# Second messages of a graph network: gathering features by chunk, and passing them through DRAM

## The chip, the cores and the metric

The kernel runs on one core of a Trainium2 chip. The metric is the device time of one execution in microseconds, lower is better. Engines: PE multiplies matrices, DVE (vector), ACT (scalar) and POOL (GpSimd) work on tiles, SP issues transfers. Sixteen DMA engines move data between DRAM and on-chip tiles; queue q1 is SP's, q10 ACT's, q0 POOL's.

## The reference

Two graph layers run over 12500 nodes with 160 features each (64 scalars and 32 vectors of three) and 212500 edges. The second one, cut to its messages:

```python
w = relu(edge_feature @ W_fc1) @ W_fc2            # (E, 224), five blocks
xs, xv = s[dst], v[dst]                           # gathered features: 64 and 32x3
tp = concat([w0 * xs, w3 * dot(xv, sh1), (w1 * xs) x sh1, w2 * xv, w4 * cross(xv, sh1)])
agg = segment_sum(tp, src, num_segments=N) / 32   # (N, 480)
```

Then `agg` goes through small matrices, a skip term and gates, and is added to x.

## The kernel before

Earlier stages sort the edges by the node that they are summed into. For each edge they leave one row of 229 words in `sorted_rows1` in DRAM (224 weights, three of direction, the key, and the index of the node whose features it needs), and for each node one row of 160 words in `feat_tab1`. After sorting, the rows of a block of 128 nodes lie together.

`messages(nc, t, l, g)` is used for both layers; the change is for the second, `L1`. It works in 928 steps (`NST`). A step takes 256 rows (`ST`), two for each of 128 partitions, from a row that a table names (`first_row`): a step never mixes blocks, so steps start at rows that aren't multiples of 256, and at the latest at 256 times their number. The steps are written out in turns of 12 (`TURN`), and a loop goes over the turns.

- SP (`group`): once in four steps (`GROUP`) it waits until the accumulation that is 8 steps back is done, reads four first rows from the table, and issues four loads of 256 rows into `rows`, a ring of 12 (`HELD`). Each load's pattern is given through `lanes(..., WIDE_LANES)`, which puts a dimension of 8 outermost.
- POOL (`gather`, L1506): for each step it waits for the rows and for a free slot in `feat`, a ring of 6 (`RING`), and issues two indirect DMAs of 128 rows of 640 B from `feat_tab1`, one for each of the step's two rows of a partition, with the indices in the rows.
- DVE: makes a one-hot matrix of the node within the block (L1790), one step later multiplies weights with features into `prod` (L1800, L1807), and adds PE's result to the accumulator (L1865) two steps after that.
- ACT: scales the one-hot by the three components of the direction (L1622), and issues stores of finished blocks to `agg_tab` (L1701) when a flag in a table says so.
- PE: 16 matmuls a step, scaled one-hots times products (L1601).

In code, the parts that the change touches:

```python
def lanes(a, n):
    return a.rearrange("(b a) w -> a b w", a=n)

sp.dma_start(rows[slot][:, :, :],
             lanes(g.sorted_rows[l.n][bass.ds(first[n], ST), :].rearrange(
                 "(p k) w -> p (k w)", k=ST_TILES), WIDE_LANES)).then_inc(rows_here[slot], 16)
```

Of the kernel before, what the change touches and what calls it, by code (L numbers as in the profile page):

```python
# [18 lines left out]
F32 = mybir.dt.float32  # L19
# [32 lines left out]
HELD = 12  # L52
GROUP = 4
TABLE_AT = 32
STORE_LAG = 10
NST = N_EDGES // ST + NBLK
HST = NST // 2
# [11 lines left out]
DIGITS = 6  # L69
TABLE_STEPS = 18  # L70
WIDE_LANES, SMALL_LANES = 8, 4
assert TURN % GROUP == 0 and NST % GROUP == 0 and HELD % GROUP == 0
assert PER_TURN % 2 == 0 and MID % 2 == 0 and NBLK + BLOCK_LAG <= MID_STEPS + 2 and NCHUNK % SLOTS == 0
assert NHI * NLO >= NBIN and NCOL % PIECE == 0
# [73 lines left out]
def build(nc, t, out):  # L148
    est = ExitStack()
    g = Shared()  # L150
    with est:
        def sb(name, shape, dt, ctx=est):
            return ctx.enter_context(nc.sbuf_tensor(name, shape, dt))

        def sem(name, ctx=est):
            return ctx.enter_context(nc.semaphore(name))

        def dram(name, shape, dt):
            return nc.dram_tensor(name, shape, dt, kind="Internal").ap()

        g.ps = [est.enter_context(nc.psum_tensor(f"bank{i}", [P, 512], F32)) for i in range(2)]
        g.ps2 = [est.enter_context(nc.psum_tensor(f"pair{i}", [P, 2, 512], F32)) for i in range(3)]

        g.sorted_rows = [dram(f"sorted_rows{l.n}", (E_PAD, l.width), I32) for l in (L0, L1)]
        g.feat_tab = [dram(f"feat_tab{l.n}", (N_PAD, D), F32) for l in (L0, L1)]
        g.agg_tab = [dram(f"agg_tab{l.n}", (N_TAB, l.agg), F32) for l in (L0, L1)]
        g.skip_tab = dram("skip_tab", (N_PAD, sum(L1.skip_cols)), F32)


        g.x_sb = sb("x_sb", [P, NBLK, D], F32)  # L170
        g.attr_s = sb("attr_s", [P, 3, NBLK], F32)
        g.ident = sb("ident", [P, P], F32)
        g.iota_n = sb("iota_n", [P, P], F32)
        g.ones_f = sb("ones_f", [P, P], F32)
        g.lower_bf = sb("lower_bf", [P, P], BF16)
        g.upper_bf = sb("upper_bf", [P, P], BF16)
        g.iota_bin = sb("iota_bin", [P, NBIN], BF16)
        g.tri = sb("tri", [P, CHUNK_TILES, CHUNK_TILES], BF16)
        g.before_f = sb("before_f", [P, P], F32)
        g.upto_f = sb("upto_f", [P, P], F32)  # L180
        g.eps = sb("eps", [P, 1], F32)
        g.w1 = [sb(f"fc1_{l.n}", [2 * l.fc_in, P], F32) for l in (L0, L1)]
        g.w2 = [sb(f"fc2_{l.n}", [P, l.wnum], F32) for l in (L0, L1)]
        g.wn_s = [sb(f"node_s{l.n}", [S0, S0 + l.skip_cols[0]], F32) for l in (L0, L1)]
        g.wn_v = [sb(f"node_v{l.n}", [V0, V0 + l.skip_cols[1]], F32) for l in (L0, L1)]
        g.w_out = [sb(f"w_out{l.n}", [P, len(l.kchunks), l.out_cols], F32) for l in (L0, L1)]
        g.neg_cross = sb("neg_cross", [32, 32], F32)
        fields = sb("fields", [TABLE_AT + 1, -(-(NST + STORE_LAG) // GROUP) * GROUP, 2], I32)
        g.first_row = fields[0:1, :, :].rearrange("p u c -> p (u c)")[:, 0:NST]
        g.table = fields[TABLE_AT:TABLE_AT + 1, :, :]  # L190
        g.fields = fields
        g.base_node = sb("base_node", [P, NST], F32)
        g.same_block = sb("same_block", [P, NST], F32)
        g.count_c = [sb(f"count_c{n}", [NHI * NLO, 1], F32) for n in range(2)]
        g.bin_start = [sb(f"bin_start{n}", [1, NBIN], F32) for n in range(2)]


        g.hi1 = sb("hi1", [P, NCOL + CHUNK_TILES], BF16)

        g.passed = sem("passed")  # L200
        g.feat_here = [[sem(f"feat_here{s}_m{l.n}") for s in range(RING)] for l in (L0, L1)]
        g.rows_sent = [sem(f"rows_sent{s}") for s in range(SLOTS)]
        g.sent = [[sem(f"sent{h}_{where}") for h in range(2)] for where in ("m0", "c")]
        sort_edges(nc, t, g)
        messages(nc, t, L0, g)
        middle(nc, t, g)
        messages(nc, t, L1, g)
        node_sums1(nc, out, g)

# [1196 lines left out]
def messages(nc, t, l, g):  # L1406
# [3 lines left out]
    with ExitStack() as ctx:  # L1410
# [3 lines left out]
        def sem(name):  # L1414
            used.append(nc.alloc_semaphore(f"{name}_m{l.n}"))
            return used[-1]

        sends = l.n == 0
        rows = [sb(f"rows{s}", [P, ST_TILES, l.width], I32) for s in range(HELD)]
        feat = [sb(f"feat{s}", [P, ST_TILES, D], F32) for s in range(RING)]  # L1420
        hot = [sb(f"hot{s}", [P, ST_TILES, 1 if sends else 4, P], F32) for s in range(l.hot_bufs)]
        prods = l.prod_bufs
        prod = [sb(f"prod{s}", [P, ST_TILES, l.pw], F32) for s in range(prods)]
        acc = [sb(f"acc{s}", [P, l.agg], F32) for s in range(l.accs)]
        rows_here = [sem(f"rows_here{s}") for s in range(HELD)]
        feat_here = g.feat_here[l.n]
        acc_stored = [sem(f"acc_stored{s}") for s in range(l.accs)]
        hot_ready, hot_scaled, prod_ready, sum_ready, acc_ready, iota_made = (
            sem(x) for x in ("hot_ready", "hot_scaled", "prod_ready", "sum_ready", "acc_ready", "iota_made"))
        if sends:  # L1430
            part = [sb(f"part{s}", [P, ST_TILES, S0 + V0], F32) for s in range(2)]
            part_ready, inner_ready, outer_ready = (sem(x) for x in ("part_ready", "inner_ready", "outer_ready"))
            scaled, made = outer_ready, inner_ready
            later = [sb(f"later{h}", [P, CHUNK_TILES, L1.width], I32) for h in range(2)]
            meta = [sb(f"meta{h}", [P, CHUNK_TILES, L1.meta], I32) for h in range(2)]
            turned = [sb(f"turned{h}", [2 * L1.fc_in, HALF * P], F32) for h in range(2)]
            hT = [sb(f"hT{h}", [P, HALF * P], F32) for h in range(2)]
            place = [sb(f"place{h}", [P, CHUNK_TILES], I32) for h in range(2)]
            sq = sb("sq", [P, CHUNK_TILES, 3], F32)
            dist = [sb(f"dist{n}", [P, CHUNK_TILES], F32) for n in range(3)]  # L1440
            turned_here = [sem(f"turned_here{h}") for h in range(2)]
            meta_here = [sem(f"meta_here{h}") for h in range(2)]
            sent = g.sent[0]
            hid_ready, hT_ready, w_ready, evicted, norm, root_ready, inverse, copied = (
                sem(x) for x in ("hid_ready", "hT_ready", "w_ready", "evicted", "norm", "root_ready", "inverse", "copied"))
            iota = g.ps2[1][:, 1, 0:P]
            r = rank_buffers(L1, sb, sem, g, g.ps2[2][:, 0, :], g.hi1, place, PER_TURN, iota=iota[:, 0:NBIN])
            hid = g.ps2[2][:, 1, :]
            w_bank = {i: g.ps2[0][:, n % 2, :] for n, i in enumerate(PAIRS)}
            res = [b[:, 0:l.agg].rearrange("p (o c) -> p o c", o=1)  # L1450
                   for b in (g.ps[0], g.ps[1], g.ps2[1][:, 0, :])]
        else:
            scaled, made = hot_scaled, prod_ready
            iota = g.ps[0][:, 0:P]
            res = [g.ps2[2 - s][:, :, 0:l.agg // 2] for s in range(l.res_bufs)]
# [23 lines left out]
        def _(sp):  # L1479
            def group(step, it, s):  # L1480
# [9 lines left out]
                for n in range(GROUP):  # L1490
# [1 line left out]
                    sp.dma_start(rows[slot][:, :, :],  # L1492
                                 lanes(g.sorted_rows[l.n][bass.ds(first[n], ST), :].rearrange(
                                     "(p k) w -> p (k w)", k=ST_TILES), WIDE_LANES)).then_inc(rows_here[slot], 16)
            turns(sp, STEPS, TURN, group, upto=NST // TURN)

        @block.gpsimd
        def _(pool):
            def gather(step, it, s):
                u = it * TURN + s  # L1500
                pool.wait_ge(rows_here[s % HELD], 16 * (use(it, s, HELD) + 1))
                if step is None or step >= RING:
                    pool.wait_ge(prod_ready, u - RING + 1)
                settle(pool, g.passed)
                for k in range(ST_TILES):
                    pool.indirect_dma_start(  # L1506
                        out=feat[s % RING][:, k, :], out_offset=None, in_=g.feat_tab[l.n],
                        in_offset=bass.IndirectOffsetOnAxis(ap=rows[s % HELD][:, k, l.idx_at:l.idx_at + 1], axis=0)
                    ).then_inc(feat_here[s % RING], 16)

            def send(step, it, s):

# [13 lines left out]
                        in_=later[h][:, k, :], in_offset=None).then_inc(sent[h], 16)  # L1526

            def step_(step, it, s):
                if step is None or step < NST:
                    gather(step, it, s)  # L1530
                if sends and (step is None or step >= 6):
                    send(step, it, s)
            turns(pool, STEPS, TURN, step_, tail=6 if sends else 0, upto=NST // TURN)
            if sends:
                for h in range(2):
                    pool.wait_ge(sent[h], CHUNK_TILES * 16 * (NCHUNK0 // 2))
# [188 lines left out]
        def _(dve):  # L1725
# [87 lines left out]
            def first_products(step, it, s):  # L1813
                u = it * TURN + s
                w, f, scalars, vectors = forms(s)
                dve.wait_ge(feat_here[s % RING], 16 * ST_TILES * (use(it, s, RING) + 1))
                if step is None or step >= prods:
                    dve.wait_ge(sum_ready, u - prods + 1)
                if sends:
# [296 lines left out]
```

## Time and profile before

| | us |
|---|---|
| median of 3 runs | 9462.45 (9452.29 to 9468.72) |
| the profiled execution | 9444.39 |
| its span, first to last instruction | 9442.3 |
| the second messages' gathers, first to last start | 6846.8 to 9237.0 |

Busy shares over the whole span: PE 70%, DVE 76%, POOL 73%, ACT 52%. They mix stages with different limits, so the rows below are mostly of one stage.

### The profile page before, as it was taken

Reading aid. Unit: us, or ns where it says so; the run is one execution under the profiler, and the core shown is the slowest. Engines: PE = TensorE matmul, PEld = TensorE weight load, DVE = VectorE, ACT = ScalarE, POOL = GpSimd, SP = SyncE. Lnnn points to the kernel's source line nnn. Section 1 sums busy time; section 2 is a strip of 40 time slices with the busy share of each in tenths; the row PEclk is TensorE's granted clock in tenths of the full one; section 3 lists DMA queues with packets and bytes.
Section 4 is the critical chain, followed back from the end, with each engine's and each line's share of the span. In section 5 each row is a group of like instructions: output and inputs, shape, how many; then the busy total and the mean of one; then the engine's idle time right before and its main releaser. Section 6 shows DMA issues by size and latency. Waiting matters only on the chain. (4 is left out here: it accounts for less than half of the span.)

```text
span 9442.3 us, 170962 instructions
## 1 busy us (share of the span) xinstructions
PE 6603.2 (70%) x31166; PEld 4445.8 (47%) x31166; DVE 7219.4 (76%) x21240; ACT 4946.3 (52%) x16490; POOL 6911.8 (73%) x7069
## 2 busy tenths in 40 slices
PE   5666566655565555555565555578799999999999
PEld 3333333332222222222222222246588888888888
DVE  7666666665777777777777777767799999999996
ACT  3444444443444444444444444444477777777775
POOL 5777777777777777777777777766677777777771
PEclk7556555657888888888888888889899999999999
DMA  3222222224444444444444444445556666666667
GB/s 105 93 91 93 92 92 93 91 90 123 139 139 140 138 138 139 139 139 139 138 139 139 139 139 139 136 143 174 158 167 168 169 169 168 170 171 167 170 166 231
DMA packets 826471, 1315.58 MB, mean 139 GB/s; under 512 B 228521, under 2 KB 627625, under 8 KB 826281
## 3 DMA queue, kind: packets, MB, share of 16 engines
q0 software_dynamic: 337920, 667.48, 25.2%
q1 hardware_dynamic: 417496, 547.30, 19.3%
q10 hardware_dynamic: 70992, 100.14, 3.1%
q8 instruction: 20, 0.33, 0.0%
q14 instruction: 43, 0.34, 0.0%
HBM read 862.45 MB, written 914.08 MB: 188 GB/s over the span
## 5 line engine op out<-in xcount | busy, mean ns | idle before, releaser
L1506 POOL DMA_INDIRECT feat_m<-feat_tab,rows_m x3712 | 3638.3, 980 | 1155.8 <-issue 984.9
L1634 ACT ACTIVATE prod_m<-part_m,rows_m 128x64 f32<-128x64 f32 x5568 | 1432.4, 337 | 2136.1 <-DVE part_m L1824 1940.3
L1601 PE MATMUL pair<-prod_m,hot_m 128*128 128x160 f32 x14848 | 2246.6, 305 | 158.1 <-DVE prod_m L1807 121.7
L1582 PE MATMUL bank<-prod_m,hot_m 128*128 128x449 f32 x2476 | 1322.6, 665 | 1438.8 <-DVE prod_m L1844 1287.6
L1601 PEld LDWEIGHTS pair<-prod_m,hot_m 128*128 128x128 f32 x14848 | 2045.5, 190 | 359.3 <-issue 354.2
L1622 ACT ACTIVATE hot_m<-hot_m,rows_m 128x128 f32<-128x128 f32 x5568 | 1728.6, 389 | 693.6 <-DVE hot_m L1790 687.6
L659 POOL DMA_INDIRECT sorted_rows<-rows_e,place_e x1664 | 1611.1, 968 | 540.9 <-issue 505.5
L1582 PEld LDWEIGHTS bank<-prod_m,hot_m 128*128 128x128 f32 x2476 | 534.4, 231 | 2169.0 <-issue 2003.6
L1524 POOL DMA_INDIRECT sorted_rows<-later_m,place_m x1248 | 1229.5, 985 | 385.5 <-issue 371.0
L1807 DVE TENSOR_TENSOR prod_m<-rows_m,feat_m 128x192 f32<-128x192 f32 (+2 forms) x4640 | 1319.0, 323 | 0.0
L1865 DVE SCALAR_TENSOR_TENSOR acc_m<-acc_m,same_block,pair 128x640 f32<-128x640 f32 (+1 forms) x1237 | 1033.4, 835 | 3.4 <-PE pair L1601 3.4
L1824 DVE TENSOR_TENSOR part_m<-rows_m,feat_m 128x128 f32<-128x128 f32 x928 | 268.1, 289 | 939.9 <-DMA feat_m<-feat_tab,rows_m 938.1
L1800 DVE TENSOR_TENSOR prod_m<-rows_m,feat_m 128x128 f32<-128x128 f32 x2784 | 726.5, 293 | 96.0 <-DMA feat_m<-feat_tab,rows_m 94.6
L1582 PE MATMUL pair<-prod_m,hot_m 128*128 128x449 f32 x1236 | 548.8, 567 | 166.0 <-DVE prod_m L1844 165.5
L484 PE MATMUL pair<-fc,hT_e 64*128 64x192 f32 x3328 | 602.6, 539 | 0.4 <-ACT rows_e L688 0.4
L412 PE MATMUL bank<-bin_count_e,upper_bf 128*128 128x100 bf16 x207 | 53.7, 259 | 779.7 <-DVE bin_prod_e L346 779.7
L484 PEld LDWEIGHTS pair<-fc,hT_e 64*128 64x128 f32 x3328 | 500.0, 325 | 198.0 <-issue 197.9
L796 DVE COPY first_sh_e<-meta_e 128x8 f32<-128x8 f32 x208 | 35.9, 173 | 701.3 <-DMA sorted_rows<-rows_e,place_e 698.9
L1115 POOL DMA_INDIRECT sorted_rows<-later_c,place_c x416 | 425.8, 1024 | 191.2 <-issue 135.3
L686 ACT ACTIVATE rows_e<-pair,first_sh_e 128x96 f32<-128x96 f32 x1664 | 499.5, 371 | 121.5 <-PE pair L484 121.5
L676 ACT ACTIVATE hT_e<-bank 128x512 f32<-128x512 f32 x208 | 124.2, 597 | 701.5 <-PE bank L929 700.4
L1790 DVE SCALAR_TENSOR_TENSOR hot_m<-pair,base_node,rows_m 128x256 f32<-128x256 f32 x928 | 445.6, 480 | 30.6 <-issue 21.4
(263 smaller groups left out, 9893.8 us busy)
## 6 DMA issues: line engine op xcount, KB each, us to landing
agg_tab<-acc_m ACTq DMA_DIRECT2D x928, 320.0 KB
rows_m<-sorted_rows SPq DMA_DIRECT2D x928, 229.0 KB
agg_tab<-acc_m ACTq DMA_DIRECT2D x928, 224.5 KB
rows_m<-sorted_rows SPq DMA_DIRECT2D x928, 197.0 KB
feat_m<-feat_tab,rows_m POOLq DMA_INDIRECT x3712, 2.7
turned_m<-in_turned ACTq DMA_DIRECT2D x159, 256.0 KB
agg_s<-agg_tab SPq DMA_DIRECT2D x98, 320.0 KB, 4.0
sorted_rows<-rows_e,place_e POOLq DMA_INDIRECT x1664, 2.4
```

The costliest lines, as they stand in the source:

```text
L484: return pe.matmul(out, hT[h, k % HALF * P:(k % HALF + 1) * P], g.w2[l.n][h, :], start=True, stop=True)
L659: pool.indirect_dma_start(out=g.sorted_rows[0], out_offset=bass.IndirectOffsetOnAxis(ap=place[s][:, k:k + 1], axis=0), in_=rows[s][:, k, : ...
L686: act.activation(rows_f[:, 2 * i + k, 0:96], w[:, k, 0:96], ACT.Copy, scale=first_sh[s][:, 2 * i + k, :])
L1506: pool.indirect_dma_start(out=feat[s % RING][:, k, :], out_offset=None, in_=g.feat_tab[l.n], in_offset=bass.IndirectOffsetOnAxis(ap=rows[s ...
L1524: pool.indirect_dma_start(out=g.sorted_rows[1], out_offset=bass.IndirectOffsetOnAxis(ap=place[h][:, k:k + 1], axis=0), in_=later[h][:, k, ...
L1582: mm = pe.matmul(out[:, 0, :], hot[s % l.hot_bufs][:, k, 0, :], prod[s % prods][:, k, 0:l.agg], start=(k == 0), stop=(k == ST_TILES - 1))
L1601: mm = pe.matmul(dst, hot[s % l.hot_bufs][:, k, q, :], rhs, start=(k == 0 and q < 2), stop=(k == ST_TILES - 1), skip_group_check=True)
L1622: ins = act.activation(hot[s % l.hot_bufs][:, k, 1 + q, :], hot[s % l.hot_bufs][:, k, 0, :], ACT.Copy, scale=rows[s % HELD][:, k, l.sh_at ...
L1634: ins = act.activation(prod[s % prods][:, k, at:at + S0], part[s % 2][:, k, 0:S0], ACT.Copy, scale=rows[s % HELD][:, k, l.sh_at + m:l.sh_a ...
L1800: return dve.tensor_tensor(out_p[:, :, pcol:pcol + 64 * d].rearrange("p k (q c) -> p k q c", q=2)[:, :, :, 0:32], w[:, :, wcol:wcol + 64]. ...
L1807: return dve.tensor_tensor(out_p[:, :, pcol:pcol + 32 * d * n].rearrange("p k (m c) -> p k m c", m=n)[:, :, :, 0:32], w[:, :, wcol:wcol + ...
L1865: dve.scalar_tensor_tensor(half(acc[q]), half(prev), same, res[s % l.res_bufs], ALU.mult, ALU.add).then_inc(acc_ready, 1)
```

## The change

In the second layer POOL no longer gathers features for each step's own rows. The sorted rows, padded to 212992, are cut into 208 chunks of 1024 rows at multiples of 1024. For each chunk SP loads the 1024 indices (one word out of each row of 229), POOL gathers 8 x 128 feature rows with them, SP puts the result to `feat_sorted` in DRAM, in sorted order, and each step then loads its 256 feature rows from there with the same first row as its rows. Three chunks are in work at a time (`AHEAD`), chunk n + 1 is put down in the group of four steps that loads up to chunk n, and `feat` becomes a ring of 12. The first layer is as before.

```diff
+AHEAD = 3
+AHEAD_TURNS = (NCHUNK - AHEAD) // AHEAD
+        g.feat_sorted = dram("feat_sorted", (E_PAD, D), F32)
-        sends = l.n == 0
+        sends, staged = l.n == 0, l.n == 1
-        feat = [sb(f"feat{s}", [P, ST_TILES, D], F32) for s in range(RING)]
+        feat = [sb(f"feat{s}", [P, ST_TILES, D], F32) for s in range(HELD if staged else RING)]
+        if staged:
+            index = [sb(f"index{s}", [P, CHUNK_TILES], I32) for s in range(AHEAD)]
+            fetched = [sb(f"fetched{s}", [P, CHUNK_TILES, D], F32) for s in range(AHEAD)]
...
 # SP, in group(), after the four loads of rows
+                if not staged:
+                    return
+                q = s // GROUP
+                n_ = it * AHEAD + q
+                if step is None or n_ + AHEAD < NCHUNK:
+                    load_index(n_ + AHEAD, q)
+                if step is None or n_ < NCHUNK:
+                    sp.wait_ge(put_down[q], 16 * (it + 1))
+                for n in range(GROUP):
+                    slot = (s + n) % HELD
+                    sp.dma_start(feat[slot][:, :, :],
+                                 lanes(g.feat_sorted[bass.ds(first[n], ST), :].rearrange(
+                                     "(p k) w -> p (k w)", k=ST_TILES), WIDE_LANES)).then_inc(feat_here[slot], 16)
+                if step is None or n_ + 1 < NCHUNK:
+                    put(n_ + 1, it + (q + 1) // AHEAD, (q + 1) % AHEAD)
+
+            def put(n, it, q):
+                sp.wait_ge(fetched_here[q], CHUNK_TILES * 16 * (it + 1))
+                sp.dma_start(g.feat_sorted[bass.ds(n * CHUNK, CHUNK), :].rearrange("(p k) w -> p k w", k=CHUNK_TILES),
+                             fetched[q][:, :, :]).then_inc(put_down[q], 16)
+
+            def load_index(n, q):
+                sp.dma_start(index[q][:, :].rearrange("p (k o) -> p k o", o=1), g.sorted_rows[l.n][bass.ds(n * CHUNK, CHUNK), l.idx_at:l.idx_at + 1].rearrange(
+                    "(p k) o -> p k o", k=CHUNK_TILES), allow_slow_non_contiguous=True).then_inc(index_here[q], 16)
+            if staged:
+                for n in range(AHEAD):
+                    load_index(n, n)
+                put(0, 0, 0)
...
 # POOL
+            def fetch(it, q, first=False):
+                pool.wait_ge(index_here[q], 16 * (it + 1))
+                if not first:
+                    pool.wait_ge(put_down[q], 16 * it)
+                settle(pool, g.passed)
+                for k in range(CHUNK_TILES):
+                    pool.indirect_dma_start(
+                        out=fetched[q][:, k, :], out_offset=None, in_=g.feat_tab[l.n],
+                        in_offset=bass.IndirectOffsetOnAxis(ap=index[q][:, k:k + 1], axis=0)).then_inc(fetched_here[q], 16)
             def step_(step, it, s):
+                n = it * AHEAD + s // GROUP + AHEAD
+                if staged:
+                    if s % GROUP == 0 and (step is None or n < NCHUNK):
+                        fetch(it + 1, s // GROUP)
...
 # DVE, in first_products()
+                if staged:
+                    dve.wait_ge(feat_here[s % HELD], 16 * (use(it, s, HELD) + 1))
```

## Rows read from the trace of the kernel before

**Rows 1.** The page: DVE, DMA busy tenths in 40 slices

```profile
DVE  7666666665777777777777777767799999999996
...
DMA  3222222224444444444444444445556666666667
```

**Rows 2.** Windows, 6860 to 9200: busy us by engine, clock, DMA share, GB/s

```profile
6860.00:9200.00 2340.00, 2197.13 (x14535) 1999.89 (x14534) 2251.15 (x7265) 1690.37 (x5445) 1786.53 (x1817) 1.00 0.62 168
```

**Rows 3.** One line, L1506, 6840 to 9240: count, ns min/median/max, first and last start

```profile
L1506 POOL DMA_INDIRECT feat_m<-feat_tab,rows_m x1856: 942/946/1637, 6846.8 to 9237.0; - x186
```

**Rows 4.** Groups by line and form, 6860 to 9200: busy us, mean ns, idle before

```profile
L1506 POOL DMA_INDIRECT feat_m<-feat_tab,rows_m x1817 | 1787.7, 984 | 553.8 <-issue 426.4 <-DMA rows_m<-sorted_rows 63.7 <-DVE prod_m L1807 63.7
...
L1865 DVE SCALAR_TENSOR_TENSOR acc_m<-acc_m,same_block,pair 128x640 f32<-128x640 f32 x909 | 807.0, 888 | 1.5 <-PE pair L1601 1.5
```

**Rows 5.** Waits, 6860 to 9200: us in total, times, longest us

```profile
POOL feat_m L1506 <- issue: 426.4, 1399, 0.5
...
PE pair L1601 <- DVE prod_m L1807: 107.1, 129, 2.0
DVE prod_m L1800 <- DMA feat_m<-feat_tab,rows_m: 86.7, 115, 1.9
POOL feat_m L1506 <- DMA rows_m<-sorted_rows: 63.7, 209, 0.3
```

**Rows 6.** Timeline, 8000 to 8012: start, us, engine, line

```profile
8003.84 0.89 DVE L1865 SCALAR_TENSOR_TENSOR acc_m<-acc_m,same_block,pair 128x640 f32<-128x640 f32 x1
...
8005.56 3.10 SPq L1492 DMA_DIRECT2D rows_m<-sorted_rows  x4
...
8006.30 0.89 DVE L1865 SCALAR_TENSOR_TENSOR acc_m<-acc_m,same_block,pair 128x640 f32<-128x640 f32 x1
```

**Rows 7.** DMA queues, 7200 to 8800: packets, MB, share of 16 engines; issues

```profile
q1 hardware_dynamic: 84336, 145.43, 29.9%
q0 software_dynamic: 59595, 101.75, 28.8%
q10 hardware_dynamic: 9792, 22.29, 3.6%
...
rows_m<-sorted_rows SPq DMA_DIRECT2D x622, 229.0 KB
feat_m<-feat_tab,rows_m POOLq DMA_INDIRECT x1242
```

**Rows 8.** Timeline, the stage's start

```profile
6841.95 11.82 SPq L1492 DMA_DIRECT2D rows_m<-sorted_rows  x12
6845.94 0.48 DVE L1790 SCALAR_TENSOR_TENSOR hot_m<-bank,base_node,rows_m 128x256 f32<-128x256 f32 x1 [3.07 <-DMA rows_m<-sorted_rows]
...
6853.65 0.49 DVE L1800 TENSOR_TENSOR prod_m<-rows_m,feat_m 128x128 f32<-128x128 f32 x2 [5.72 <-DMA feat_m<-feat_tab,rows_m]
```

**Rows 9.** Windows of 1 us at the stage's start

```profile
6844.00:6845.00 1.00, 0.00 (x0) 0.00 (x0) 0.00 (x0) 0.00 (x0) 0.00 (x0) 0.50 0.52 178
...
6847.00:6848.00 1.00, 0.00 (x0) 0.00 (x0) 0.48 (x1) 1.00 (x5) 0.76 (x1) 0.50 0.52 167
```

**Rows 10.** DMA queues and issues, 500 to 1500, the first sort

```profile
q0 software_dynamic: 37728, 79.33, 23.0%
...
sorted_rows<-rows_e,place_e POOLq DMA_INDIRECT x787, 2.4
```

**Rows 11.** DMA queues, 34 to 60, small loads of weights

```profile
q1 hardware_dynamic: 2224, 0.24, 6.4%
```

**Rows 12.** DMA queues and issues, 9300 to 9400, the last stage (last column: us to landing)

```profile
q1 hardware_dynamic: 23430, 27.55, 92.3%
...
agg_s<-agg_tab SPq DMA_DIRECT2D x54, 320.0 KB, 4.0
```

**Rows 13.** Windows, 2000 to 6600, the first messages

```profile
2000.00:6600.00 4600.00, 2789.06 (x9023) 1360.85 (x9023) 3354.70 (x9726) 2071.64 (x7392) 3455.85 (x3517) 0.84 0.47 138
```

**Rows 14.** The page: DMA issues, us to landing

```profile
feat_m<-feat_tab,rows_m POOLq DMA_INDIRECT x3712, 2.7
```

More of the change, by code:

```diff
@@ L71 @@
 WIDE_LANES, SMALL_LANES = 8, 4
+assert TURN == GROUP * AHEAD and CHUNK == GROUP * ST
 assert TURN % GROUP == 0 and NST % GROUP == 0 and HELD % GROUP == 0
@@ L200, in build @@
         g.passed = sem("passed")
-        g.feat_here = [[sem(f"feat_here{s}_m{l.n}") for s in range(RING)] for l in (L0, L1)]
+        g.feat_here = [sem(f"feat_here{s}_m0") for s in range(RING)]
         g.rows_sent = [sem(f"rows_sent{s}") for s in range(SLOTS)]
@@ L1425, in messages @@
         rows_here = [sem(f"rows_here{s}") for s in range(HELD)]
-        feat_here = g.feat_here[l.n]
+        feat_here = [sem(f"feat_here{s}") for s in range(HELD)] if staged else g.feat_here
         acc_stored = [sem(f"acc_stored{s}") for s in range(l.accs)]
@@ L1429, in messages @@
             sem(x) for x in ("hot_ready", "hot_scaled", "prod_ready", "sum_ready", "acc_ready", "iota_made"))
+        if staged:
+            index = [sb(f"index{s}", [P, CHUNK_TILES], I32) for s in range(AHEAD)]
+            index_here = [sem(f"index_here{s}") for s in range(AHEAD)]
+            fetched = [sb(f"fetched{s}", [P, CHUNK_TILES, D], F32) for s in range(AHEAD)]
+            fetched_here = [sem(f"fetched_here{s}") for s in range(AHEAD)]
+            put_down = [sem(f"put_down{s}") for s in range(AHEAD)]
         if sends:
@@ L1494, in group @@
                                      "(p k) w -> p (k w)", k=ST_TILES), WIDE_LANES)).then_inc(rows_here[slot], 16)
-            turns(sp, STEPS, TURN, group, upto=NST // TURN)
+                if not staged:
[24 more added lines that the diff above has]
+                put(0, 0, 0)
+            turns(sp, STEPS, TURN, group, upto=AHEAD_TURNS if staged else NST // TURN)
         @block.gpsimd
@@ L1528, in step_ @@
             def step_(step, it, s):
-                if step is None or step < NST:
+                n = it * AHEAD + s // GROUP + AHEAD
+                if staged:
+                    if s % GROUP == 0 and (step is None or n < NCHUNK):
+                        fetch(it + 1, s // GROUP)
+                elif step is None or step < NST:
                     gather(step, it, s)
@@ L1532, in step_ @@
                     send(step, it, s)
-            turns(pool, STEPS, TURN, step_, tail=6 if sends else 0, upto=NST // TURN)
+            if staged:
+                for n in range(AHEAD):
+                    fetch(0, n, True)
+            turns(pool, STEPS, TURN, step_, tail=6 if sends else 0, upto=AHEAD_TURNS if staged else NST // TURN)
             if sends:
@@ L1815, in first_products @@
                 w, f, scalars, vectors = forms(s)
-                dve.wait_ge(feat_here[s % RING], 16 * ST_TILES * (use(it, s, RING) + 1))
+                if staged:
+                    dve.wait_ge(feat_here[s % HELD], 16 * (use(it, s, HELD) + 1))
+                else:
+                    dve.wait_ge(feat_here[s % RING], 16 * ST_TILES * (use(it, s, RING) + 1))
                 if step is None or step >= prods:
```

## The prediction

> **What bounds the kernel now.** I read the page first, for where the second messages lie: its slices turn near slice 29 of 40 (6,850 us): DVE goes from seven tenths to nine, the DMA engines to six, until slice 39 [rows 1]. Then the windows of that stage: DVE and PE are busy for over nine tenths and POOL for three quarters, so by shares POOL would be the last to look at, and the DMA share of 0.62 looks harmless [rows 2]. The groups by line and the waits choose. POOL ran 1856 gathers from 6846.8 to 9237.0 us [rows 3], 1.289 us each. In the stretch 6860 to 9200 it has 1787.7 us busy and 553.8 us idle for 1817 of them, 0.984 and 0.305 us, and no single idle stretch is over 0.5 us, whoever is named as releaser [rows 4, 5]. The 0.30 us is thus the gap between any two gathers: POOL never stops. DVE waits 86.7 us for gathered features, and PE 107.1 us for DVE's products [rows 5]. So POOL paces: two gathers a step, 2.58 us. DVE is close behind: when it isn't held, its L1865 starts every 2.46 us [rows 6]; its busy time is 2251 us for 909 steps, 2.48 each. At most 0.1 us a step could come from a freer POOL.
>
> The DMA share hides the tightest thing. From 7200 to 8800, q1 (SP's rows loads) moved 84336 packets for 622 issues, about 620 of them landing inside it, q10 9792 packets with 22.29 MB of 327.68 KB stores, 68 stores, and q0 59595 for 1242 gathers [rows 7]. That is 144 packets a store, the 128 rows and 16 small ones; and 136 a rows load, 128 and 8. One small packet closes the work of each DMA engine, so a rows load runs on eight engines, a store on sixteen. Are they always the same eight? At the stage's start SP issues twelve rows loads 1 us apart [rows 8], more than eight engines drain, and until gathers land, the DMA share stands at 0.52 in four windows of 1 us in a row, at 178 down to 162 GB/s (the first and the last are shown) [rows 9]. Loads queue up while half of the engines stand idle: the same eight each time. I call them the lanes.
>
> The lanes' load, per engine. q1: 29.9% of 16 engines over 1600 us is 7654 us, on eight engines 957 us. q0: 28.8% is 461 us on each engine. q10: 3.6%, 58 us. Sum 1476 of 1600 us: the lanes are 92% busy where the mean of all says 62%.
>
> **The change, part by part.** The unit is a group of four steps and one chunk: 232 groups, the first 208 with a chunk. A group now takes 4 x 2.58 = 10.3 us.
>
> *Gathers.* 1856 become 1664, but they stay eight for each of the first 208 groups: 8 x 1.289 = 10.3 us, POOL's pace as before. Only in the last 24 groups is it free. The waits of POOL (the index landed, the put of three chunks before) stand once a chunk before eight gathers; three buffers put them two chunks ahead. A wait of such a kind shows no idle time of its own now [rows 5]. Alone this would give 208 x 10.3 + 24 x 4 x 2.46 = 2145 + 236 = 2381 us against 2391.5 for the 1856 gathers now. Nothing.
>
> *Transfers on the lanes for a group, per engine.*
> - Rows loads, kept: 7654 / 620 = 12.35 us of engine time, over 8 is 1.54, times 4 = 6.17 us. Lower bound from the queued start: 234.5 KB at 178 GB/s is 1.32 us [rows 9], 5.27 for four.
> - Gathers, kept: 461 us / 1242 = 0.371, times 8 = 2.97 us. Lower bound: the first sort's scatters of 788 B rows, 23.0% of 16 x 1000 us for 787 [rows 10], 0.292 each, 2.34.
> - Stores, kept: 58 us in 155 groups, 0.37.
> - Feature loads, new: four a group, `lanes(..., WIDE_LANES)` around 256 rows of 640 B, the rows load's own pattern with other widths, so the same eight engines. 163.8 KB at the rows loads' price per byte (7654 us / 145.43 MB = 52.6 us per MB) is 8.62 us, over eight 1.08; four are 4.31 us. Below: 163.8 KB at 178 GB/s, 3.68. Above: a packet of 1280 B costs what one of 1832 B does, 90.8 ns, so 16 x 4 x 90.8 = 5.8. I take 4.31; a packet of some 100 B costs 12 ns (6.4% of 16 x 26 us for 2224 packets) [rows 11], so the size carries most of the price.
> - The put, new: 655 KB with 128 partitions outermost like the stores, so 16 engines: 41.4 us per MB (922 / 22.29) gives 27.1, over 16 is 1.69 us. Above, at the price of the saturated last stage (92.3% of 1600 us for 27.55 MB, 53.6 per MB) [rows 12]: 2.2.
> - The index load, new: 1024 single words, 916 B apart, also 128 partitions outermost: 64 a engine. At 12 ns 0.77 us. Above: what a gathered row at a random place costs, 0.371 us / 8 = 46 ns, gives 2.97. I take 0.8: a word moves as little as the small packets.
>
> Sum: 6.17 + 2.97 + 0.37 + 4.31 + 1.69 + 0.80 = 16.31 us a group, where POOL needs 10.3 and DVE 9.84. With all lower bounds 14.0, with all upper ones 20.5. **The lanes become the bound.** Do they stay busy? While SP waits for a put, they have the four rows loads and the index load queued behind it (some 7 us of work), more than the tail of a landing (4.0 us for a 320 KB load in all [rows 12]). SP's own work a group is 8 loads of 0.78 us and two smaller issues, 7.5 us [rows 6], and behind its waits there is nothing for others but these loads. The wait for `acc_ready` reaches 8 steps back, over 30 us at the new pace. So I use the sum as the pace.
>
> The Trainium skill, "DMA: Bandwidth & Descriptors", section "Why a DMA increments its semaphore by 16 and not by 1", says that a hardware-generated DMA uses the largest number of engines up to 16 that divides the slowest dimension of both patterns, the lowest-numbered ones. The 136 and 144 packets and the 0.52 agree; by it the put and the index load run on 16. Were the put confined to the lanes as the loads are, against that rule, it would cost 3.38 us of them, 18.0 a group and some 350 us more in all. The same page, "Rules for kernel authors", has a strided last dimension lowered to one descriptor per element; that speaks against the index load, and no trace of before shows one.
>
> *The last 24 groups* have rows, features and stores: 6.17 + 4.31 + 0.37 = 10.85 us, just over DVE's 9.84: 260 us.
>
> *The start.* Now the first product comes at 6853.65, 11.7 us after the first rows load [rows 8]. Then: an index lands in 4 us (as the first rows do), eight gathers 10.3, landing 2.7 [rows 14], the put about 4.8, a feature load 4: 26, so +15 us. Nothing covers it.
>
> *Sum.* 208 x 16.31 + 260 + 15 = 3668 us against 2391.5: +1276. The profiled execution took 9444.4 us (span 9442.3), so 10,720; the median of the runs lies 18 us above it: 10,740. PE would be busy some 60% in bursts; the first messages run so at a mean clock of 0.84 [rows 13], which makes 2.4 us of matmuls a step (2197 us for 908 steps of 16 [rows 2]) 2.9, below the new 4.1 us a step. The lower clock is covered.
>
> **Rivals.**
> - *The index load is dear.* 46 ns a word: +2.17 us a group, +450 us: 11,190. For it: each word is a place of its own in DRAM. Against: small packets at 12 ns. 13 in 100.
> - *The new loads spread over all engines*, or packets shrink under load. With everything on sixteen: 0.62 x 10.3 = 6.4, plus 2.16, 1.69, 0.8 = 11.05 a group: 208 x 11.05 + 236 + 15 = 2549, +158: 9,620. Against: the share of 0.52 with loads queued. 7 in 100.
> - *It changes nothing*: POOL still paces, eight gathers a chunk. This needs the lanes to do a group within 10.3 us. 9,460. Against: they have 0.8 us free a group, and 6.8 us are added. 3 in 100.
> - *The other side: faster.* Features arrive as loads, DVE never waits for a gather and runs at 2.46 us a step: 928 x 2.46 + 15 = 2298, -93: 9,370. It needs POOL at 1.23 us a gather, and the lanes below 9.84 us a group; for it speaks only that DVE's waits for features are the stage's bottleneck today. 2 in 100.
> - *Forecast*: lanes bound at 14.0 to 17.8 us a group (17.8 with the upper price of the feature loads), 10,230 to 11,080. 75 in 100.
>
> **How the numbers follow.** The range 10,230 to 11,200 holds the forecast's span and the dear index load at its full price; outside it are the spread case, the two others, and mixtures beyond 11,200. 0.2% (19 us) is what can be told from no change here. Faster by more: 2 in 100. Within: 3. Slower: 95.
>
> **What would show it.** DMA share over the first 208 groups: all engine time over sixteen, 11.05 / 16.31 = 0.68, with a pace of 16.3 us for eight gathers, so 0.68 looks as harmless as today's 0.62 while half of the engines are full; q1 near 128 + 8 packets for each feature load; index packets of 64 a engine near 12 ns; DVE waiting for `feat` loads some 6 us a group; POOL waiting once a chunk for `put_down`. Wrong if q1's feature loads show 144 packets each, if the group's pace is 10 to 11 us, or if SP's issue of the index load takes several us.

## The result and the profile after

The changed kernel takes 10010.63 us (median of 4, 10007.87 to 10019.78) against 9465.58 us before, a ratio of 1.0581 with a 95% interval of 1.0565 to 1.0598: 545 us slower. The forecast was 10,740 us in a range of 10,230 to 11,200. The side was right, the size was twice too large. The profiled execution has a span of 10009.7 us, 567 more than before. (The table of experiments compares each run with runs of the kernel before made beside it, whose median was 9445 to 9450 us; ratios are therefore safer to compare than differences of times.)

The page of the changed kernel, DVE and DMA in 40 slices, against [rows 1]:

```profile
DVE  7666666657777777777777776776777777777796
...
DMA  3222222234444444444444444556777777777757
```

From slice 29 to 38 the DMA engines are at seven tenths instead of five to six, and DVE stays at seven where it went to nine. The same stretch in windows, with the line of the new gathers (count, ns min/median/max, first and last start; POOL's share of busy time is 1433 of 2340 us), against [rows 2, 3]:

```profile
6860.00:9200.00 2340.00, 1854.58 (x11419) 1752.87 (x11420) 1788.48 (x5716) 1332.74 (x4295) 1433.20 (x1454) 0.90 0.75 235
...
L1555 POOL DMA_INDIRECT fetched_m<-feat_tab,index_m x1664: 940/947/1609, 6861.0 to 9537.0; - x185
```

A chunk takes (9537.0 - 6861.0) / 208 = 12.87 us. Before, four steps took 10.3 us; the forecast was 16.3. This spacing is the measure of all runs below: it comes from the first and the last gather's start and leaves out the stage's start and end. The waits, 7000 to 9500, against [rows 5]:

```profile
POOL fetched_m L1555 <- DMA index_m<-sorted_rows: 534.7, 183, 5.3
PE pair L1656 <- DVE prod_m L1862: 482.3, 192, 4.7
DVE prod_m L1855 <- DMA feat_m<-feat_sorted: 457.6, 190, 4.5
```

POOL now really stands still, once a chunk, 2.9 us, and by the profile for the index, a load of 4 KB. The timeline shows why so small a load is late, and what SP does:

```profile
8000.16 0.59 SPq L1527 DMA_DIRECT2D index_m<-sorted_rows  x1
...
8001.80 5.53 SPq L1515 DMA_DIRECT2D feat_m<-feat_sorted  x4
...
8007.63 0.35 SPq L1523 DMA_DIRECT2D feat_sorted<-fetched_m  x1
8008.92 3.15 SPq L1502 DMA_DIRECT2D rows_m<-sorted_rows  x4
8009.44 0.94 POOL L1555 DMA_INDIRECT fetched_m<-feat_tab,index_m  x1 [2.76 <-DMA index_m<-sorted_rows]
...
8012.29 0.58 SPq L1527 DMA_DIRECT2D index_m<-sorted_rows  x1
...
8015.23 4.96 SPq L1515 DMA_DIRECT2D feat_m<-feat_sorted  x4
```

The index issued at 8000.16 releases POOL at 8009.44, 9 us later; the four rows loads of the same group went into q1 just before it. The put that POOL also has to wait for can't be what held it: SP had waited for the same put before it issued the feature loads at 8001.80. Four feature loads take SP 5.5 us to issue, where four rows loads take 3.1. Two readings fit this. Either the engines are full and everything queues (my forecast). Or SP's own order sets the pace: a put at 8007.63, the feature loads 7.6 us later when it has landed, 5.0 us to issue them, then the next put. That sum is also 13 us, and the experiments had to tell the two apart.

DMA queues, 7200 to 8800, against [rows 7]:

```profile
DMA packets 335946, 376.97 MB, mean 236 GB/s; under 512 B 155174, under 2 KB 297432, under 8 KB 335946
## 3 DMA queue, kind: packets, MB, share of 16 engines
q1 hardware_dynamic: 280735, 278.25, 52.9%
q0 software_dynamic: 47419, 80.98, 19.5%
q10 hardware_dynamic: 7792, 17.74, 2.9%
```

### The profile page after: what moved, and what is told of

Same layout as the page of the kernel before. It is cut to its first block and busy times, and to the rows that moved or that the text cites. A ratio compares the mean times of both kernels' runs of the same rounds, so it can differ in the third digit from the quotient of the medians.

```text
span 10009.7 us, 173158 instructions
## 1 busy us (share of the span) xinstructions
PE 6757.2 (68%) x31166; PEld 4652.1 (46%) x31166; DVE 7235.0 (72%) x21240; ACT 4949.5 (49%) x16490; POOL 6739.5 (67%) x6877
## 5 line engine op out<-in xcount | busy, mean ns | idle before, releaser
L1656 PE MATMUL pair<-prod_m,hot_m 128*128 128x160 f32 x14848 | 2391.2, 322 | 560.4 <-DVE prod_m L1862 541.7
L1656 PEld LDWEIGHTS pair<-prod_m,hot_m 128*128 128x128 f32 x14848 | 2250.7, 206 | 701.0 <-issue 494.2
L1555 POOL DMA_INDIRECT fetched_m<-feat_tab,index_m x1664 | 1640.3, 986 | 1048.6 <-DMA index_m<-sorted_rows 569.8
L1544 POOL DMA_INDIRECT feat_m<-feat_tab,rows_m x1856 | 1819.4, 980 | 577.3 <-issue 550.9
L1862 DVE TENSOR_TENSOR prod_m<-rows_m,feat_m 128x192 f32<-128x192 f32 (+2 forms) x4640 | 1285.6, 309 | 0.0
L1923 DVE SCALAR_TENSOR_TENSOR acc_m<-acc_m,same_block,pair 128x640 f32<-128x640 f32 (+1 forms) x1237 | 1018.5, 823 | 119.1 <-PE pair L1656 115.1
```

The source lines that it names most:

```text
L1544: pool.indirect_dma_start(out=feat[s % RING][:, k, :], out_offset=None, in_=g.feat_tab[l.n], in_offset=bass.IndirectOffsetOnAxis(ap=rows[s ...
L1555: pool.indirect_dma_start(out=fetched[q][:, k, :], out_offset=None, in_=g.feat_tab[l.n], in_offset=bass.IndirectOffsetOnAxis(ap=index[q][: ...
L1656: mm = pe.matmul(dst, hot[s % l.hot_bufs][:, k, q, :], rhs, start=(k == 0 and q < 2), stop=(k == ST_TILES - 1), skip_group_check=True)
L1862: return dve.tensor_tensor(out_p[:, :, pcol:pcol + 32 * d * n].rearrange("p k (m c) -> p k m c", m=n)[:, :, :, 0:32], w[:, :, wcol:wcol + ...
L1923: dve.scalar_tensor_tensor(half(acc[q]), half(prev), same, res[s % l.res_bufs], ALU.mult, ALU.add).then_inc(acc_ready, 1)
```

## Experiments

Three theories. *Lanes*: the eight engines that all eight-way loads share are full. *Chain*: SP's order put, landing, feature loads, put. *Bytes*: 236 GB/s is what memory gives to such traffic. "Chunk" is the time from the first gather to the last, over 208, as above.

| run | time, us | ratio to before, 95% interval | chunk, us |
|---|---|---|---|
| the changed kernel | 10010.6 | 1.0581 (1.0565 to 1.0598) | 12.87 |
| e1 both loads sixteen ways | 9495.0 | 1.0053 (1.0033 to 1.0073) | 10.47 |
| e2 put before the wait | 10004.2 | 1.0593 (1.0575 to 1.0611) | 12.89 |
| e3 feature loads sixteen ways | 9828.3 | 1.0405 (1.0388 to 1.0423) | 12.01 |
| e5 an eighth of the index | 9905.8 | 1.0488 (1.0471 to 1.0506) | 12.38 |
| e6 put twice | 10327.6 | 1.0930 (1.0912 to 1.0949) | 14.45 |
| e7 half of the gathers | 9774.3 | 1.0352 (1.0335 to 1.0370) | 11.78 |
| e8 e1 and e2 together | 9516.2 | 1.0075 (1.0058 to 1.0092) | 10.56 |
| e9 put eight ways | 10395.6 | 1.0997 (1.0980 to 1.1014) | 14.75 |
| e10 e1 with an eighth of the index | 9449.0 | 1.0000 (0.9991 to 1.0010) | 10.32 |
| e4 before, rows of layer 2 sixteen ways | 9430.1 | 0.9981 (0.9971 to 0.9991) | - |
| e11 before, rows of both layers so | 9437.7 | 0.9987 (0.9978 to 0.9996) | - |

**e1, both loads cut sixteen ways.**

```diff
-                                 lanes(g.sorted_rows[...], WIDE_LANES)
+                                 lanes(g.sorted_rows[...], 16 if l.n else WIDE_LANES)
-                                 lanes(g.feat_sorted[...], WIDE_LANES)
+                                 lanes(g.feat_sorted[...], 16)
```

> The changed kernel, with the patterns of both loads of the second layer (rows and features) cut sixteen ways instead of eight, so that each runs on sixteen DMA engines; the bytes, the order and the waits stay. Lanes theory (eight engines are full, 12.9 us a group of four steps): the engine time of 0.75 x 12.9 x 16 is spread, 9.7 us a group on each engine, so POOL's eight gathers, 10.3 us, pace again: 9,440 to 9,520 us. Chain theory (SP waits for the put's landing, then issues four feature loads, then the next put, one after the other, 13 us): nothing of that order changes, so over 9,900 us unless the landing itself was only queueing. Bytes theory (236 GB/s is what the memory gives to such traffic): the same bytes, 10,010 us.

It took 9495.0 us: the change's cost falls from 5.8% to 0.5%, with the same bytes and the same order of SP. The landing of a put is no shorter (8004.19 to 8012.15, 8.0 us, against 7.6), but the loads behind it are issued in 2.7 us:

```profile
8004.19 0.36 SPq L1523 DMA_DIRECT2D feat_sorted<-fetched_m  x1
8005.20 0.94 POOL L1555 DMA_INDIRECT fetched_m<-feat_tab,index_m  x1 [0.30 <-issue]
8005.58 2.78 SPq L1502 DMA_DIRECT2D rows_m<-sorted_rows  x4
...
8012.15 2.71 SPq L1515 DMA_DIRECT2D feat_m<-feat_sorted  x4
```

The queues in 7200 to 8800 have a surprise:

```profile
DMA packets 424341, 466.26 MB, mean 291 GB/s; under 512 B 200907, under 2 KB 376558, under 8 KB 424341
## 3 DMA queue, kind: packets, MB, share of 16 engines
q1 hardware_dynamic: 355988, 343.93, 81.1%
q0 software_dynamic: 58571, 100.07, 23.2%
q10 hardware_dynamic: 9782, 22.26, 3.7%
```

291 GB/s, so 236 was no limit of memory; and shares that add up to 108%. A share over 100% is possible only if packets of one engine overlap: their times, added, are then longer than the time that passes. And a byte of q1 costs more engine time here: 52.9% of 25600 us for 278.25 MB is 48.7 us per MB in the changed kernel, here 81.1% for 343.93 MB is 60.4. The traces' packet records of the same window, taken by size, say which packets those are: the mean for a rows packet (1832 B) goes from 84.6 to 105.8 ns, for a feature packet (1280 B) from 59.5 to 84.8, while a put's packet (5120 B) stays at 201 to 202.

**e2, the put ahead of the wait.**

```diff
+                if step is None or n_ + 1 < NCHUNK:
+                    put(n_ + 1, it + (q + 1) // AHEAD, (q + 1) % AHEAD)
                 if step is None or n_ < NCHUNK:
                     sp.wait_ge(put_down[q], 16 * (it + 1))
...
-                if step is None or n_ + 1 < NCHUNK:
-                    put(n_ + 1, it + (q + 1) // AHEAD, (q + 1) % AHEAD)
```

> The changed kernel, with the put of chunk n + 1 issued before SP waits for the put of chunk n and issues the feature loads, so that no put waits for the landing of the one before. Lanes theory: the same transfers on the same full engines, 9,980 to 10,030 us. Chain theory: the chain is cut, POOL's 10.3 us a group pace, 9,450 to 9,560 us. Bytes theory: 10,010 us.

10004.2 us, a chunk 12.89: no change. The chain theory falls: SP's waits add up to 14 us in 7000 to 9200, so nothing that SP waits for sets the pace. The delay only moved into the issue of the put, as its line shows (median 3910 ns, where the changed kernel has 546):

```profile
L1523 SPq DMA_DIRECT2D feat_sorted<-fetched_m x208: 335/3910/5976, 6858.8 to 9533.6; - x104
```

**e3, only the feature loads sixteen ways** (the second `lanes` of e1; a partition then multiplies features of other rows of its step).

> The changed kernel, with only the feature loads cut sixteen ways; the rows loads stay on eight engines. The partitions then get the features of other rows of the same step, so the messages are not the reference's. Lanes theory: of 3.8 us of feature packets a group on the lanes half goes, 12.9 becomes 11.0 us, about 9,600 us. Chain theory: 10,000 us, or as much less as the put's landing shortens. Bytes theory: 10,010 us.

9828.3 us, a chunk 12.01. The direction is that of the lanes theory, the size less than half: 0.86 us instead of 1.9. Its queue 1 in 7200 to 8800:

```profile
q1 hardware_dynamic: 306118, 299.51, 61.8%
```

That is 52.8 us per MB against 48.7: part of what the lanes lost in packets came back as dearer packets. By the packet records they were the features': their mean goes from 59.5 to 74.7 ns, that of the rows only from 84.6 to 86.1.

**e5, an eighth of the index.**

```diff
-                sp.dma_start(index[q][:, :]...
+                sp.dma_start(index[q][:, 0:w]...            # w = 1 after the first three chunks
```

> The changed kernel; after the first three chunks an index load brings 128 of a chunk's 1024 indices, the other 896 stay those of the buffer's first chunk, so the features aren't the reference's. What it takes off each lane is 56 single words a chunk. Additive lanes at the packets' measured price (9 ns a word, engine time counted 1.07 times over): 0.47 us a group, 98 us in all, 9,910. By my forecast's upper price (46 ns a word) 2.4 us a group, 9,500. If words cost the lanes nothing: 10,010.

9905.8 us against 9,910 expected. 56 words fewer on each engine save 0.49 us a chunk, 8.7 ns a word, so the whole index load of 64 costs 0.56 us. The packet records have 9.0 ns for a word. The price from the run isn't quite clean, since most of the gathers now read the same rows of the table again and the gathers' packets come out some 6% cheaper.

**e6, the put twice.**

```diff
                              fetched[q][:, :, :]).then_inc(put_down[q], 16)
+                sp.dma_start(g.feat_again[bass.ds(n * CHUNK, CHUNK), :]...,
+                             fetched[q][:, :, :]).then_inc(put_again[q], 16)
```

> The changed kernel with a second, unused put of each chunk to another place in DRAM, right behind the first; POOL also waits for it before it fills the buffer again. Additive lanes: 8 packets of 5120 B at 201 ns on each engine, 1.6 us over 1.07, +1.5 us a group, +312 us: 10,320. Bytes theory (12.9 us are the 3.05 MB of a group): 655 KB more are +2.8 us a group, +575 us: 10,585. Chain theory (already weak): 10,010 to 10,050.

(POOL also waits for the second put before it fills the buffer again; these waits add up to 4 us.) It took 10327.6 us, a chunk 14.45: +1.58 us. The lanes' sum was met within 8 us, the bytes theory missed by 257.

**e7, half of the gathers.**

```diff
-                for k in range(CHUNK_TILES):
+                for k in range(CHUNK_TILES if first else 4):
```

> The changed kernel; after the first three chunks POOL issues four of a chunk's eight gathers, the other half of the buffer stays, so half of the features are of other rows. POOL has then 5.2 us of work a group. What a gather costs a lane: by the forecast's price, the mean over all engines of 0.371 us, four are 1.5 us less a group, -290 us (over 1.07): 9,720. If on the lanes its rows cost only their shortest packets (172 + 32 + 9 ns, what the sum leaves for them), 0.8 us, -165 us: 9,845. If POOL or the gathers' landing paced the kernel after all, more: below 9,600.

(The put waits for the smaller count.) 9774.3 us, a chunk 11.78: 1.09 us for four gathers, 0.27 each, between the two prices. POOL had little more than half of its work and the kernel still took 3.5% more than before, so POOL doesn't pace the changed kernel. The waits in 7000 to 9200:

```profile
POOL fetched_m L1555 <- DMA index_m<-sorted_rows: 1224.2, 185, 7.9
```

**e9, the put eight ways.**

```diff
-                sp.dma_start(g.feat_sorted[...].rearrange("(p k) w -> p k w", k=CHUNK_TILES),
+                sp.dma_start(lanes(g.feat_sorted[...].rearrange("(p k) w -> p (k w)", k=CHUNK_TILES), WIDE_LANES),
```

> The changed kernel with the put's pattern cut eight ways like the loads (its rows land in another order, so features aren't the reference's). Lanes theory, if the put then runs on the same eight engines as the loads: 16 packets of 5120 B a chunk on each of them instead of 8, +1.5 us a group, +310 us: 10,320, the same as the second put, at fewer bytes. The share of all DMA engines should fall while the time rises. If eight-way transfers were spread over other engines too: 10,010.

10395.6 us, a chunk 14.75, +1.88 where +1.5 was expected, so the time is 76 us over the expectation. Windows, 7200 to 8800: first the run with two puts (e6), then this one.

```profile
7200.00:8800.00 1600.00, 1192.30 (x7040) 1142.04 (x7040) 1110.97 (x3521) 819.34 (x2640) 880.36 (x880) 0.88 0.79 255
```

```profile
7200.00:8800.00 1600.00, 1183.24 (x6912) 1140.12 (x6912) 1091.70 (x3458) 804.52 (x2592) 871.26 (x865) 0.86 0.67 206
```

Both are slower than the changed kernel by more than 300 us, one at a share of 0.79 and 255 GB/s, the other at 0.67 and 206, below the changed kernel's 0.75 and 236. Neither share nor bytes tell the time. That transfers cut eight ways share the same eight engines does: had they spread, e9 would have stayed at 10,010.

**e8, sixteen ways and the put ahead** (both diffs).

> Both loads cut sixteen ways and the put issued ahead of the wait for the one before. In the run with sixteen ways alone a chunk took 10.5 us, POOL 8 x 1.31. If POOL paces there (or the full engines, whose share is 1.08), this stays at 9,480 to 9,500 us. If there SP's chain paces (landing of the put 7.9 us, then 2.7 us of feature loads, 10.6 together), it drops to POOL's 10.3 us: 9,455 us. It doesn't get under the kernel before by more than 0.2% in any case, since POOL has eight gathers for four steps in both.

9516.2 us, a chunk 10.56, 16 us over the upper end of what was expected and no faster than e1: SP's chain doesn't pace the sixteen-way version either. POOL has no idle time but its gaps and 32 us; it is the gathers that got slower, 1.32 us each.

```profile
L1555 POOL DMA_INDIRECT fetched_m<-feat_tab,index_m x1207 | 1190.0, 986 | 410.4 <-issue 378.5 <-DMA index_m<-sorted_rows 31.9
```

**e10, sixteen ways with an eighth of the index.**

> Both loads cut sixteen ways, and after the first three chunks an eighth of the index words (features then aren't the reference's). It takes 0.5 us a chunk off every engine. If in the sixteen-way version POOL paces, with gathers slowed from 1.29 to 1.31 us by full engines, little changes: 9,455 to 9,495 us. If the full engines pace, down to POOL's 10.3 us a group: 9,455. Both are near; what tells is the mean spacing of the gathers, and whether POOL waits.

9449.0 us, a chunk 10.32, 1.290 us a gather, and the ratio is 1.0000. With a little taken off the engines (their packet times add up to 106% instead of 108%) POOL is back at the pace of [rows 3]. So e1 stood close to both limits at once: POOL paces, and its gathers come some 0.02 us apart more.

**e4 and e11, the kernel before with its rows loads sixteen ways**, in the second layer (e4) and in both (e11).

> The kernel before, with the rows loads of the second layer cut sixteen ways. If POOL alone paces there (two gathers of 1.289 us a step), it stays within 0.2% of 9,465 us. If the 92% busy lanes held gathers back, the stage drops towards the 2.46 us a step of DVE, by up to 100 us: 9,370 us.

> The kernel before with the rows loads of both layers cut sixteen ways. The second layer alone gave 0.9981. The first messages are POOL's too (two gathers and their share of the sends), their lanes less full, so at most as much again: 9,410 to 9,435 us against 9,447; if the first layer has nothing to gain, 0.998 as before.

e4 took 9430.1 us, ratio 0.9981: the first to last gather went from 2390.2 us [rows 3] to 2369.0.

```profile
L1506 POOL DMA_INDIRECT feat_m<-feat_tab,rows_m x1856: 942/946/1617, 6853.0 to 9222.0; - x186
```

e11 took 9437.7, 0.9987. So spreading the rows loads brings the gathers 0.01 us each closer together, and no gain of the first layer shows: the two ratios' intervals overlap. e4 is the fastest kernel of this study, 0.2% under the kernel before, and it is that kernel with one number changed.

## Why the forecast was right in kind and twice too large

**That POOL's gathers pace the kernel before, eight for four steps with or without the change**: right. e10 has the changed order of work with less to do for the engines, and comes to a ratio of 1.0000.

**That rows and feature loads share the same eight engines and these become the bound**: right. The put doubled, the put moved to eight engines, the index cut and the loads spread all move the time with the lanes' work (e1, e3, e5, e6, e9), while SP's order (e2) does nothing and halving POOL's work (e7) gives only its packets' worth.

**The sum of 16.31 us a group taken as the pace**: this step failed. Four terms, the last column from the runs' chunks:

| term | forecast | measured | from |
|---|---|---|---|
| index load | 0.80 | 0.56 | e5, 0.49 for 56 of 64 words |
| put | 1.69 | 1.58 | e6 |
| eight gathers | 2.97 | 2.18 | e7, 1.09 for four |
| rows, features, stores | 10.85 | 8.55 | 12.87 less the three above |
| sum | 16.31 | 12.87 | the changed kernel |

Two thirds of the miss, 2.3 of 3.44 us, is in the loads. I priced them by packet times from the kernel before (7654 us for 620 rows loads) and took the sum for elapsed time. Both parts of that failed, and the packet records tell them apart. I redid the forecast's sum with the packet times of the changed kernel: what an engine of the lanes has to do for a chunk, if puts, index words, gathers and stores lie evenly on all sixteen engines and cost the same on each. The same was done for the other runs, all in 7200 to 8800:

| run | lanes' packet times, us a chunk | chunk in the window, us | the first over the second |
|---|---|---|---|
| before (four steps) | 9.52 | 10.32 | 0.92 |
| the changed kernel | 14.35 | 12.91 | 1.11 |
| e2 put before the wait | 14.42 | 12.97 | 1.11 |
| e3 feature loads sixteen ways | 13.08 | 12.03 | 1.09 |
| e5 an eighth of the index | 13.56 | 12.46 | 1.09 |
| e6 put twice | 16.08 | 14.55 | 1.11 |
| e7 half of the gathers | 12.97 | 11.85 | 1.09 |
| e9 put eight ways | 16.23 | 14.81 | 1.10 |

First, packets were cheaper than forecast: 14.35 us instead of 16.31. A rows packet fell from 95.8 ns before to 84.6, a feature packet took 59.5 where the price per byte had made it 67, a gather 0.315 us of each engine instead of 0.371. Second, these 14.35 us fit into 12.9, because packets of full engines overlap. So about 2.0 of the 3.44 us are cheaper packets and 1.5 are overlap. All seven runs that the lanes bound have nearly the same overlap, 1.09 to 1.11, at chunks from 11.9 to 14.8 us, and e3 with its dearer feature packets is among them.

The lower bound of 14.0 (its terms add up to 14.1) was none. Its gathers were a sum of packet times too. Its rows and feature loads rested on 178 GB/s of eight engines with loads queued [rows 9], and that wasn't the most that they move: the 8.55 us, less 0.37 for the stores, are 195 GB/s for the same bytes. The overlap could hardly be read from the trace of before: in none of its stretches shown do packet times add up to more than 93% of the engines' time.

**The last 24 groups at 10.85 us, lanes bound**: wrong, and small. They run at DVE's pace, L1923 every 2.46 us or 9.84 a group, some 236 us instead of 260, with q1 at 48.1% of sixteen engines, which is 96% of eight. In the changed kernel:

```profile
9599.40 0.86 DVE L1923 SCALAR_TENSOR_TENSOR acc_m<-acc_m,same_block,pair 128x640 f32<-128x640 f32 x1
9601.86 0.86 DVE L1923 SCALAR_TENSOR_TENSOR acc_m<-acc_m,same_block,pair 128x640 f32<-128x640 f32 x1
...
q1 hardware_dynamic: 22213, 32.64, 48.1%
```

There 9.5 us of q1's packets a group fit into 9.84 us, where 10.5 were forecast.

**The start, +15 us**: right. The first index load goes out at 6857.71, the first product comes at 6885.45, 27.7 us against 11.7: +16.

**PE's lower clock covered**: right as far as it was seen. The granted clock is 0.90 in the stage, a step takes 3.2 us, and PE waits for DVE's products (482.3 us), not the other way round, but for 104 us of waits of L1923 for PE.

**The rivals.** The case of all loads spread over sixteen engines was priced at 9,620, and e1 did just that, at 9495: there POOL was the bound, not the mean engine's 11.05 us, which again was a sum of packet times. The dear index load (46 ns a word) is refuted by e5: 8.7 ns. The Trainium skill ("DMA: Bandwidth & Descriptors", "Why a DMA increments its semaphore by 16 and not by 1") has the number of engines follow from the slowest dimension; by that rule the put runs on sixteen engines and e9's on eight. The runs agree: e9 costs 1.88 us a chunk, against 1.69 forecast for such a put.

**What I said the profile would show**: q1's packets came as said, eight small ones for a feature load. The chunk took 12.87 us instead of 16.3. The DMA share is 0.75 instead of 0.68: the engines had less to do than forecast (9.7 us a chunk on the mean, not 11.05), but in still less time. SP took 5.0 to 5.5 us to issue four feature loads, not 3.1. DVE waits 2.4 us a group for features instead of 6. POOL waits once a chunk, but by the profile for the index, not for `put_down`.

What stays open: why a rows packet got cheaper when the eight engines were full (95.8 to 84.6 ns) and dearer on sixteen (105.8 in e1, and 104.9 in e4, whose engines were far from full), and whether the even spread that the table assumes is exact. No record here names the engine of a packet.

## What to carry to other kernels

Before adding transfers, count packets per transfer: rows plus one small packet for each engine used says on how many engines it runs, and the mean DMA share hides eight nearly full engines behind 0.62 before, and eight full ones behind 0.75 after. If a pattern's outermost dimension confines a load to half of the engines, widen that first (here it brought the cost from 5.8% to 0.5%); then ask whether the new path relieves what paces at all, and here it didn't: the gathers stayed eight for four steps. And turn packet times into elapsed time only with a full engine's measured overlap, here 1.1. A price worked out from the changed kernel's own packets and that overlap (then taken as 1.07) foretold the second put within 8 us and e9 within 76, where the sum from the trace of before was off by 730.

## What the runs showed of the hardware

- Packet times of full DMA engines add up to more than the time: 108% of sixteen engines at 291 GB/s (e1), and 109 to 111% of eight by the sum above (the changed kernel, e2, e3, e5, e6, e7, e9).
- Load packets from DRAM were dearer with sixteen engines streaming than with eight: 105.8 against 84.6 ns for 1832 B, 84.8 against 59.5 for 1280 B (e1 against the changed kernel). In the kernel before, cutting the rows loads sixteen ways took their packets from 95.8 to 104.9 (e4). The puts' packets of 5120 B into DRAM took 202 ns in e1 against 201, though 224 in e8.
- Single words of 4 B, 916 B apart in DRAM, cost 8.7 ns each on an engine (e5; 9.0 by the packet records), less than the 12 ns of small packets of about 100 B [rows 11].
- SP's issue of the same transfer takes longer or shorter by what stands before it: four feature loads 5.5 us in the changed kernel and 2.7 us in e1; one put 0.35 us at 8007.63 in the changed kernel and 3.9 us at the median in e2, where it follows the rows and index loads at once. That SP is held by a full queue is the likely reading; no view shows how full it is.
- POOL's gathers come 1.31 or 1.32 us apart instead of 1.289 where the packet times of the engines add up to 108% (e1, e8), though the median of one stays at 0.946 us; at 106% (e10) they come 1.290 apart.
